# Grouping the value products of an attention stage, and moving the side jobs around them

## The reference, cut to what matters

```
x = x + proj(attention(layernorm_over_channels(x)))      # 8 heads of 24, q and k L2-normalised, softmax over 1024 keys
t = tokens of x
t = t + sum over the 2 best of 4 experts of gate * (gelu(LN(t) @ w1 + b1) @ w2 + b2)
```

## Time and profile before

| what | value |
|---|---|
| median of 3 runs | 2733.79 us (2733.28 to 2739.15) |
| the profiled execution | 2741.01 us, span 2739.1 us |
| attention of the 16 images | 108.5 to 1653.0 us of the span |
| expert stage, output stage | 1705 to 2672 us, 2672 to 2739 us |
| PE busy over the span | 2465.8 us (90%) |
| ACT busy over the span | 1780.7 us (65%) |

### The profile page before, as it was taken

The page is one execution under the profiler, slowest core; times in us unless marked ns, Lnnn a source line. Parts: engine busy times, 40 slices in busy tenths (PEclk is TensorE's granted clock), DMA queues, the critical chain, the costliest instruction groups (busy, mean ns, idle before and its releaser), DMA issues. The chain is left out here.

```text
span 2739.1 us, 58873 instructions
## 1 busy us (share of the span) xinstructions
PE 2465.8 (90%) x18693; PEld 1295.9 (47%) x18693; DVE 1683.5 (61%) x4886; ACT 1780.7 (65%) x2228; POOL 1420.5 (52%) x1137
## 2 busy tenths in 40 slices
PE   3699999999989999989999973999999999999975
PEld 2333333333333333333333321777777777777754
DVE  6557766866766766676676655555555555555522
ACT  2487777777778777767777852555565556555542
POOL 2334435534543543543454323677777777777750
PEclk9799999999999999999999987999999999999987
DMA  4221112112112111211211243444444444444429
GB/s 91 58 51 41 50 49 58 48 42 54 51 44 60 48 49 47 58 41 45 59 48 45 77 162 128 179 155 155 177 155 162 169 155 170 160 158 174 153 79 332
DMA packets 160322, 276.49 MB, mean 101 GB/s; under 512 B 21568, under 2 KB 129584, under 8 KB 150624
## 3 DMA queue, kind: packets, MB, share of 16 engines
q1 hardware_dynamic: 141648, 245.37, 27.8%
q0 software_dynamic: 13392, 27.97, 2.8%
q10 hardware_dynamic: 5056, 0.42, 0.3%
HBM read 174.07 MB, written 49.69 MB: 82 GB/s over the span
## 5 line engine op out<-in xcount | busy, mean ns | idle before, releaser
L788 ACT ACTIVATE probs<-ps_s 128x1024 f32<-128x1024 f32 x1024 | 1011.9, 1023 | 282.6 <-PE ps_s L687 260.0
L1360 POOL TENSOR_TENSOR h_split<-h_f,h_split 128x512 f16<-128x512 f32 x444 | 550.7, 1241 | 238.3 <-ACT h_f L1337 231.0
L1333 ACT ACTIVATE h_split<-ps_h,packs 128x512 f16<-128x512 f32 x444 | 305.2, 687 | 391.1 <-PE ps_h L1287 368.8
L1287 PE MATMUL ps_h<-m_xn_t,packs 128*128 128x512 f16 x2220 | 552.4, 380 | 0.5 <-DVE m_xn_t L1422 0.5
L700 PE MATMUL ps_o<-probs,v_aug 128*32 128x512 f32 x4096 | 550.6, 610 | 0.4 <-ACT probs L788 0.4
L1054 POOL TENSOR_TENSOR inv_norm<-sumsq,minus_half 128x16 f32<-128x16 f32 x128 | 378.0, 2953 | 312.4 <-DVE sumsq L997 307.6
L1301 PE MATMUL ps_y<-packs,h_split 128*128 128x192 f16 x5328 | 511.9, 245 | 0.9 <-POOL h_split L1360 0.9
L1301 PEld LDWEIGHTS ps_y<-packs,h_split 128*128 128x128 f16 x5328 | 453.0, 97 | 105.7 <-POOL h_split L1360 1.9
L687 PE MATMUL ps_s<-stacks_odd 98*128 98x512 f16 x1024 | 301.5, 386 | 17.0 <-DMA stacks_odd<-heads 10.2
L687 PE MATMUL ps_s<-even 98*128 98x512 f16 x1024 | 299.0, 383 | 11.6 <-ACT probs L788 5.7
L1337 ACT ACTIVATE h_f<-ps_h,packs 128x512 f32<-128x512 f32 x444 | 302.0, 680 | 0.0
(11 more groups left out here) (213 smaller groups left out, 2812.6 us busy)
## 6 DMA issues: line engine op xcount, KB each, us to landing
packs<-expert_pack SPq DMA_DIRECT2D x74, 1635.0 KB, 6.6
even<-heads SPq DMA_DIRECT2D x192, 96.0 KB, 2.4
stacks_odd<-heads SPq DMA_DIRECT2D x192, 96.0 KB, 2.4
tile_rows<-sorted_rows SPq DMA_DIRECT2D x37, 400.0 KB
tokens<-in_x_dram SPq DMA_DIRECT2D x17, 768.0 KB, 5.3
y_in<-y_tokens SPq DMA_DIRECT2D x16, 768.0 KB, 8.9
out_dram<-y_out SPq DMA_DIRECT2D x16, 768.0 KB, 7.1
even<-heads SPq DMA_DIRECT2D x128, 48.0 KB
```

Of the source, the lines that this page charges most:

```text
L788: act.activation(probs[:, u % PRING, :], ps_s[:, u % 2, :, :].rearrange("p f n -> p (f n)"), ACT.Exp).then_inc(s_probs, 1)
L1287: mm = pe.matmul(ps_h[:, n % HBUF, :], w1(par, slot, w, k), xn_t[0:rows_k, par, c, :], start=(i == 0), stop=(i == 4))
L1333: act.activation(h_split[:, n % HSPLIT, 0, :], ps_h[:, n % HBUF, :], ACT.Gelu, bias=bias1(par, slot, k), scale=1.0 / WSCALE)
L1360: pool.tensor_tensor(h_split[:, n % HSPLIT, 1, :], h_f32[:, n % HBUF, :], h_split[:, n % HSPLIT, 0, :], ALU.subtract).then_inc(s_h, 1)
```

## The change

The two calls of `pv` for one key block stand together, in units 1, 5, 9, ... (every fourth), and in such a unit the jobs come first, then the scores of the next unit are made ahead, then the two calls. (In unit 1, whose calls belong to the image before, the scores of unit 2 are not made ahead.) The second copy out of the accumulators moves one unit forward. The rounds stand every 4 units from 14 to 50 instead of every 4.5 to 55, and the 24 output jobs get a list of units written out, 14 of which stand in the last 14 units (50 to 63).

```diff
-PV_AT = range(1, UNITS, 2)
-TAKE_AT = (2, 4)
+PV_AT = range(1, UNITS, GH)
+TAKE_AT = (2, 3)
...
-ROUNDS = tuple(14 + (9 * r + 1) // 2 for r in range(NT + 2))
-POST_UNITS = tuple(19 + 44 * i // (3 * NT - 1) for i in range(3 * NT))
+ROUNDS = tuple(14 + GH * r for r in range(NT + 2))
+POST_UNITS = (20, 24, 28, 30, 32, 36, 40, 42, 44, 48, 50, 51, 52, 54, 55, 56, 58, 59, 60, 61, 62, 62, 63, 63)
...
         for u in range(UNITS):
-            if attend:
+            if attend and not (u - 1 in PV_AT and u - 1 >= PV_LAG):
                 scores(pe, img, par, u)
-            if u in PV_AT and u >= PV_LAG and attend:
-                pv(pe, img, par, (u - PV_LAG) // 2)
-            elif u in PV_AT and u < PV_LAG and has_post(img):
-                pv(pe, img - 1, 1 - par, PVS + (u - PV_LAG) // 2)
             for job in jobs_at(img, u):
                 pe_job(pe, img, par, n, job)
                 n += 1
+
+            if u in PV_AT and u >= PV_LAG and attend:
+                scores(pe, img, par, u + 1)
+                for f in range(2):
+                    pv(pe, img, par, (u - PV_LAG) // 2 + f)
+            elif u in PV_AT and u < PV_LAG and has_post(img):
+                for f in range(2):
+                    pv(pe, img - 1, 1 - par, PVS + (u - PV_LAG) // 2 + f)
```

## The result

The changed kernel takes 2828.6 us (median of four runs, 2828.1 to 2829.9) against 2735.4 for the kernel before: ratio 1.0347, 95% interval 1.0334 to 1.0360. It is 93 us slower. The direction was right; 2756 us, the predicted time, and the range up to 2785 were too low.

A forecast was written before the change was run, and what follows sets the result against it. TensorE's order of work was taken as the bound, ScalarE close behind with two bank pairs. Images 3 to 14 +1, images 0, 1, 2 and 15 +7, +4, +2.5, +7: 2733.8 + 22 = 2756 us; range 2722 to 2785.

The forecast's parts named there:

- The loop: From pair to pair: pair 1.84, scores to exponential 0.64, two exponentials 1.94, 0.59 to the next pair; 5.01 us.
- the walk of an image: Sum of one steady image's cycles, each named by its pair's unit: 21.6 + 13.0 + 41.2 + 22.4 = 98.2 us.
- the guess for 17: Cycle of the pair at unit 17, with two VectorE rounds: 7.4 us taken, between ends of 5.6 and 8.2.
- 13 and 25: Cycles of the pairs at units 13 (job u behind the pair, 5.6 us) and 25 (a round with q, 6.7).
- Images 3 to 14: 12 x (98.2 - 98.1) = +1: Twelve steady images: walked 98.2 us each against the measured mean of 98.1 before, so +1 us.
- With q 7 read out some 17 us before the border ... I take it to be gone: TensorE's unit 0 stall, ascribed to SyncE's DMAs, vanishes; included in the 98.2; up to 20 us more if it stays.
- The saving: Rival: the grouping's saving comes through, TensorE's own work counts; likelier form 2719 us, in full 2655; chance 0.22.
- the draw: Rival: border and rounds give back what empty cycles cost; image at 97.2, -11 + 11 = 0, 2734 us; chance 0.13.
- The falling clock: Rival: TensorE's waits in every cycle lower its clock, once an image, +26 us, 2782 us; chance 0.10.
- Images 0 to 2 and 15: Images outside the twelve steady ones, forecast longer by 7, 4, 2.5 and 7 us.
- The low end of 96.4: Lower end for a steady image's 98.2 us: cycles 17 and 29 fully hidden, minus 1.8 us.
- the last rival: The pair is no cheaper in mid-stream than two calls; loop 0.2 us longer, +50 at most, 2800 us; chance 0.03.

The follow-up runs named there:

- full_after: The changed kernel with images 3 to 14 written out, no hardware loop over images: 2769.4 us, 1.0133 of the kernel before.
- full_before: The kernel before with images 3 to 14 written out, no hardware loop over images: 2687.5 us, 0.9827 of the kernel before.
- noahead_full: full_after with the scores of the next unit made behind the pair of value calls instead of ahead of it: 2731.1 us.
- turn4_after: The changed kernel with four images in a turn of the hardware loop, three turns instead of six: 2811.2 us, 1.0283 of the kernel before.
- group_only: The changed kernel, in its hardware loop, with the rounds and output jobs in the units of before: 2814.5 us.
- c7free_after: The changed kernel, in its hardware loop, with the last output jobs moved so that c 7 does not wait for b 7: 2827.1 us.

## Why the prediction was right in direction and wrong in size

- **The loop and the walk of an image: right.** Pair 1.92 us, cycle 5.03 for 5.01, rounds 6.7, 5.9 at 45; 98.45 us an image in full_after for 98.2. Over twelve images the walk is off by 3 us. Some of that is luck: the guess for 17 was 0.35 too long, 13 and 25 were 0.2 too short.
- **The step that failed: "Images 3 to 14: 12 x (98.2 - 98.1) = +1".** 98.1 was the mean of the kernel before *with* all that its hardware loop costs, 98.2 a sum of operations *without* it. The proper partner of the walk was 93.8. The 51.3 us that full_before shows as the loop's own were booked as if the change removed them. Of the 62.3 us missing here (63.5 less 1.2), this is 51.3; the loop's costs in the changed kernel are 8.0 higher (the stalls 6.3, the low clock about 8, the pace inside the images about 6 less); the walk's 3.0 are the rest. The rows had it: image 2, written out, took 94.0 us and image 3 96.4 with the same jobs. The prediction used that difference for image 2 alone, and there took it off the walk; image 2 then took 98.8 us, the walk's time, for 96.5.
- **"With q 7 read out some 17 us before the border ... I take it to be gone": wrong.** The profile's name for the wait was a DMA, and the earlier trace rows seemed to fit, but they show the six DMAs of L645, which unit 0 does not wait for. What was late was TensorE's own instruction stream at the branch. It did not go but grew, from 12.6 to 18.9 us in five turns. A test was at hand in the trace of before: q 7's DMAs are as late in every image (issued until 871.02 for the scores at 871.17, into image 8), and every second border has no stall.
- **The rivals.** The saving and the draw are out: TensorE's work fell and nothing came through. The falling clock came partly: stretches of 3.4 to 6.8 us at half clock after the turns, as before, and four inside images (at 634, 1334, 1464 and 1542 us). By the cycles in which they stand (8.4, 6.6, 8.3 and 7.6 us for 7.4, 5.2, 7.4 and 5.2, with the neighbours) they cost about 7 us, and those after the turns, by the lengths of the images behind them, about as much again; both are part of the 59.3. The rival had one low stretch in every image, 26 us. The Trainium skill, TensorE: Matmul & The Clock Gate, A second HAM failure mode: psum-queue depth-cycling, expects short waits between groups to make the clock oscillate; full_after has the same waits of up to 1.2 us for the exponential and a granted clock of 1.00 over images 3 to 14. So short waits mostly did not do it here, but they can stand before it: in noahead_full, written out too, a pair of image 5 ran at half clock behind waits of 0.35, 0.51 and 0.31 us, on PE:

```profile
585.20 3.46 PE L700 MATMUL ps_o<-probs,v_aug 128*32 128x512 f32 x16
```

- **Images 0 to 2 and 15: undersized.** +9.0, +4.8, +4.8, +7.9 for +7, +4, +2.5, +7, 6 us in all. The rounds of image 0 measure the 6.7 written; 1.5 of its 2 us lie before its first pair, which starts 7.4 us into the image for 5.9.
- **Sums that do not come out.** The low end of 96.4 takes off the 1.8 of cycle 17 alone; with 29 hidden too, as it says, it is 95.7. The draw's +11 is 17 by its own terms, and the last rival's 50 on 2756 is 2806, not 2800. None of them moves the forecast.

What stays open: why the clock falls inside images 3 to 14 several times in each kernel with both the loop and the grouping (the changed one, turn4_after, group_only, c7free_after), never in those without the grouping, and once in the written-out ones with it (noahead_full); and how the turn's wait depends on the queued work in numbers.

## What to carry to other kernels

Grouping calls of one engine to save its mode changes makes a block, and a block must be bridged by the buffers of the engine it feeds: with two bank pairs and two exponentials of 0.92 us a block of 1.84 us can't be (5.0 us a cycle for 4.2). Work the loop out from release to release before counting what a call saves. And compare a walk with a walk: before using it against a measured mean, walk the kernel before by the same rule, and book the difference from its mean as a cost that stays.

## What the runs showed of the hardware that was not expected

- A turn of the hardware loop over two images costs TensorE 1.7 to 4.2 us, and mostly a stretch at 1.2 GHz behind it (after four of five turns before, all five after). The profile gives the wait either to a DMA or to nothing; the DMAs that unit 0 waits for had landed over 5 us earlier (image 7 of the kernel before). The Trainium skill, Runtime: NRT & Kernel Launch, Instruction fetch mechanics, says that a taken branch whose target isn't in the fetch window stalls until it is fetched; the waits at turns alone, and none in the written-out kernels, agree. The wait is longer when TensorE's last job waits for a read-out (2.3 to 3.0 us became 3.6 to 4.1 with one job moved).
- Besides the turns, an image in the loop takes some 2.6 us more than one written out (96.4 against 93.8 before; after, 1.9 to 2.4 us). In the loop the semaphore waits go by values in registers, and the page counts 58,873 instructions for 53,823 written out. That these are the cost was not tested by itself.
- With both gone, the kernel before takes 2687.5 us, 48 less than with its loop: more than the change was about.
